# Writing the steps of a pipelined transformer stage out, and forming the product with V over 64 rows from two arrangements of V

## The chip, the core and the metric

The kernel runs on one core of a Trainium2 chip. The metric is the device time of one execution in microseconds (us), of which several runs are taken; 4808 to 4830 us is what the runs of the kernel before show. The program is written by hand for the five engines of the core: TensorE (PE, matmuls, with its weight loads as PEld), VectorE (DVE), ScalarE (ACT), GpSimd (POOL) and SyncE (SP, which issues the DMAs here). Each engine has a queue of its own, and the engines wait for each other through semaphores.

## What is computed

The reference is a chain of small networks over one input of 16 sequences of 256 tokens with 128 channels. The part that the change touches is a transformer of six layers with attention in windows of 32 tokens; a window sees its own tokens and those of the window before:

```python
def local_attention(q, k, v):            # 16 heads of 64 columns, w = 32
    ...
    bq = q.reshape(b, h, nw, w, d)
    ...
    def look(t):                         # the window before, zeros in front of a sequence
        p = jnp.pad(t, ((0, 0), (0, 0), (1, 0), (0, 0), (0, 0)))
        return jnp.concatenate([p[:, :, :nw], p[:, :, 1:]], axis=3)
    bk2, bv2 = (look(bk), look(bv))
    ...
    sim = jnp.einsum('bhwie,bhwje->bhwij', bq, bk2) * QK_SCALE
    sim = jnp.where(mask, -jnp.finfo(sim.dtype).max, sim)
    attn = jax.nn.softmax(sim, -1)
    out = jnp.einsum('bhwij,bhwje->bhwie', attn, bv2)
```

Ahead of the attention, half of the channels are shifted by one token, q and k are normalised and rotated; behind it come the output product, a residual sum, and a gated feed-forward layer. The product `bhwij,bhwje->bhwie` (probabilities by values, 64 keys for each of 32 queries) is called the product with V below. The other networks (one in front, four behind) are not touched.

## The kernel before, in words

The transformer stage works on tiles of 128 tokens: two tiles are one sequence of one layer (a unit), so that 16 sequences and 6 layers make 96 units and 192 tiles. It is a software pipeline of steps. In step k TensorE projects q and k of tile k (`project`, L1071), turns q and k of tile k-1 (`turn_part`, transposes at L1053), makes masks and scores of tile k-2 (`scores`, L1102 and L1112), projects v of tile k-2 (`project_v`, L1087), turns the probabilities of tile k-3 and forms its product with V (`attend`, L1144), and forms the output product of tile k-4 (L1167). The feed-forward layer takes two units at a time, spread over four steps (`widen` and `narrow`, L1189 and L1203). So TensorE's work repeats every four steps. VectorE rotates and makes the softmax's sums, GpSimd sums the rotated parts and scales, ScalarE squares, exponentiates and copies PSUM banks to SBUF: o of tile k-3 (`keep_out`), V of tile k-2 (`keep_v`, L1275, from the bank that the scores also use), q and k of tile k-1.

The order on each engine is written out by hand (`body(step)` of each engine). The first 16 steps and the last 16 are written out; the eleven rounds of 16 steps between run in a hardware loop (`all_steps`, L773), in which each engine's waits are against values computed in its registers from the round. `Event.at` gives such a value; `place` numbers the fills of the turning bank.

The probabilities of a tile lie in `probT` with the keys on the partitions: the 64 keys of a window at rows 0 to 63 for the even heads and 64 to 127 for the odd ones. The keys stand by their row modulo 64, so in every second window the own window is the lower half and the window before the upper half, and in the others the other way round. `V` holds the values likewise, 64 rows of two windows for even and for odd heads, in four slots for four tiles. `attend(step, parity)` works on 32 rows of V at a time: a slice of V of one window serves its own window and the next (64 moving columns), or one of them alone (32 columns) at a tile's edge. Both calls add into the same PSUM bank, which two priming matmuls with zeros (L1131) have opened. The first call (32 matmuls) stands before the transposes of k of the next tile, the second (32 for an even tile, 48 for an odd one, which has the slice of the tile before to add) behind them, with a wait for the first.

SP's queue carries, for each unit: the shifted output (`shift_output`, L897 to L899), the residual (L891), the input with its shift (L886 to L888), and every second unit the saved z (L904). At a layer's end SP loads the next layer's weights in parts and gives each free by an event (`q_ok` for the q columns, `k_ok`, `v_ok`, `out_ok` for Wo, `ff_ok`), in between waiting for their last readers.

Of the kernel before, what the change touches and what calls it, by code (L numbers as in the profile page):

```python
# [16 lines left out]
P = 128  # L17
# [652 lines left out]
LOOP = 16  # L670
# [16 lines left out]
class Step:  # L687
# [12 lines left out]
    def v_slot(self, lag):  # L700

        return (self.k - lag) % 4
# [5 lines left out]
    def has(self, lag):  # L708
        return not isinstance(self.I, int) or 0 <= self.tile(lag) < TILES

    def has_input(self):
        return self.k % 2 == 1 and (not isinstance(self.I, int) or self.tile(0) < TILES)
# [5 lines left out]
    def has_pair(self):  # L718
        return not isinstance(self.I, int) or 0 <= self.pair() < UNITS // 2
# [41 lines left out]
def place(step, name):  # L761

    if isinstance(step.I, int) and step.I == 0:
        return FIRST_FILLS[step.k, name]
    if isinstance(step.I, int) and step.I == ROUNDS:
        return LAST_FILLS[step.k, name]
# [3 lines left out]
def all_steps(engine, body):  # L770
    for k in range(LOOP):
        body(Step(0, k))
    with engine.Fori(1, ROUNDS) as I:  # L773
        for k in range(LOOP):
            body(Step(I, k))
    for k in range(LOOP):
        body(Step(ROUNDS, k))


def transformer_stage(k, z):  # L780

    nc, d = k.nc, k.dram
    with ExitStack() as ctx:
# [14 lines left out]
        zerob = sb("zerob", [P, P], BF16)  # L798
# [12 lines left out]
        V = sb("V", [P, 4, WPT // 2, PAIRS, HD])  # L811
# [38 lines left out]
        v_done, v_kept, pv_done = ev("v_done"), ev("v_kept"), ev("pv_done", 2)  # L850
# [8 lines left out]
        def _(sp):  # L859
            for e in (zu_ready, zr_ready[0], zr_ready[1], zsh_ready, z_saved, q_ok, k_ok, v_ok, out_ok, ff_ok):  # L860
                e.start(sp)
# [30 lines left out]

            def shift_output(U, unit):
# [12 lines left out]
            sp.wait_ge(zeroed, 5)  # L906
# [23 lines left out]
            def unit(U):  # L930
# [23 lines left out]
                if U:  # L954
                    sp.sem_inc(v_ok.sem, 1)
                if U + 2 <= UNITS:
# [34 lines left out]
        def _(pool):  # L991
# [7 lines left out]
            pool.wait_ge(zeroed, 4)  # L999
# [44 lines left out]
            all_steps(pool, body)  # L1044

        @block.tensor
        def _(pe):
# [13 lines left out]
            def project(step, kind):  # L1061
                tau, t = step.tile(0), step.t(0)
                if t == 0:
                    e = k_ok if kind else q_ok
                    pe.wait_ge(e.sem, e.at(step.I * (LOOP // 2) + step.k // 2, 1))
                    if kind == 0 and not (isinstance(step.I, int) and tau == 0):
# [56 lines left out]
            def attend(step, parity):  # L1123
# [1690 lines left out]
```

## Time and profile before

| | |
|---|---|
| median of 3 runs | 4816.22 us (4808.3 to 4830.12) |
| the profiled execution's own time | 4819.65 us |
| its span in the trace | 4817.9 us |
| transformer stage in the trace | about 210 to 3626 us |
| TensorE busy | 4398.4 us, 91% of the span |
| VectorE busy | 3142.6 us, 65% |
| ScalarE busy | 2723.2 us, 57% |
| GpSimd busy | 2626.5 us, 55% |

The times of single instructions come from the profiled execution, whose span begins 1.8 us short of its time. A float32 matmul leaves two records in the trace, so a group "x64" is 32 matmuls. Matmuls overlap, so what one costs is the distance from its start to the next one's start and not its own length. The granted clock of TensorE is given as a share of its full speed: 1.00 is the 2.4 GHz level, 0.50 the 1.2 GHz level. Idle time in brackets is what the engine stood still before the row, with what ended it; "issue" means that the profile shows nothing that it waited for.

### The profile page before, as it was taken

To read this page: it belongs to the slowest core of one execution; us is meant where nothing else is said; L and a number is where in the kernel's file an instruction comes from. 1 tells how busy PE (TensorE), PEld (TensorE's weight loads), DVE (VectorE), ACT (ScalarE), POOL (GpSimd) and SP (SyncE) were. 2 spreads that over 40 slices of the span, in tenths; PEclk is the share of its full clock that TensorE was granted. 3 is DMA by queue.
4 is the path that set the end of the run, shared out by engine and by line. 5 is a ranking of instruction groups with operands and counts; after the bars stand their busy time and mean duration, and the time that the engine had idled before them with its cause. 6 is when DMAs were issued, how large, how long until landed. Compare 5 with 4: busy or idle time off the path is not lost. (4 is left out here: it accounts for less than half of the span.)

```text
span 4817.9 us, 164830 instructions
## 1 busy us (share of the span) xinstructions
PE 4398.4 (91%) x72648; PEld 2863.6 (59%) x72648; DVE 3142.6 (65%) x4111; ACT 2723.2 (57%) x3930; POOL 2626.5 (55%) x1467
## 2 busy tenths in 40 slices
PE   7489999999999999999999999999984999788878
PEld 5256666666666666666666666666652555344435
DVE  3477676767667666667666676766743443599974
ACT  4246665656666565566656665665652444577743
POOL 0266665666666665666666665666632212477752
PEclk8599999999999999999999999999995999799989
DMA  2100001000100001100010001000001000211100
GB/s 55 51 11 16 19 20 37 20 20 18 30 24 25 18 18 33 27 20 15 20 37 23 17 20 29 24 24 18 19 14 33 1 1 1 87 76 71 71 34 16
DMA packets 184442, 134.16 MB, mean 28 GB/s; under 512 B 122296, under 2 KB 170433, under 8 KB 181633
## 3 DMA queue, kind: packets, MB, share of 16 engines
q1 hardware_dynamic: 183681, 122.99, 8.5%
q8 instruction: 602, 9.86, 0.9%
q14 instruction: 159, 1.30, 0.1%
HBM read 68.50 MB, written 4.03 MB: 15 GB/s over the span
## 5 line engine op out<-in xcount | busy, mean ns | idle before, releaser
L1005 POOL TENSOR_TENSOR tf_qk<-tf_qk,tf_rot 128x1024 f32<-128x1024 f32 x384 | 908.9, 2367 | 1221.8 <-DVE tf_rot L1388 1221.8
L1071 PE MATMUL tf_psum<-tf_Wqkv,tf_xsT 128*128 128x512 f32 x1536 | 749.6, 611 | 66.9 <-issue 46.5
L1012 POOL TENSOR_TENSOR tf_qk<-tf_qk,tf_rn 128x1024 f32<-128x1024 f32 x384 | 724.3, 1913 | 53.5 <-ACT tf_rn L1271 53.4
L1264 ACT ACTIVATE tf_sq<-tf_psum 128x1024 f32<-128x1024 f32 x384 | 393.4, 1025 | 533.7 <-DVE tf_rot L1388 533.7
L1384 DVE TENSOR_TENSOR tf_qk<-tf_psum,tf_table 128x1024 f32<-128x1024 f32 x384 | 467.4, 1217 | 265.3 <-PE tf_psum L1071 264.6
L1144 PE MATMUL tf_psum<-tf_probT,tf_V 32*64 32x64 f32 (+1 forms) x27648 | 494.1, 219 | 7.0 <-issue 6.6
L1071 PEld LDWEIGHTS tf_psum<-tf_Wqkv,tf_xsT 128*128 128x128 f32 x1536 | 273.4, 193 | 350.1 <-issue 339.3
L1394 DVE TENSOR_REDUCE tf_ss<-tf_sq 128x16 f32<-128x1024 f32 x384 | 457.6, 1192 | 21.3 <-ACT tf_sq L1264 21.3
L1144 PEld LDWEIGHTS tf_psum<-tf_probT,tf_V 32*64 32x64 f32 x27648 | 443.4, 133 | 45.7 <-issue 40.4
L1388 DVE TENSOR_TENSOR tf_rot<-tf_psum,tf_table 128x1024 f32<-128x1024 f32 x384 | 465.7, 1213 | 0.0
L1053 PE MATMUL tf_psum<-ident,tf_qk 128*128 128x128 f32 x3072 | 408.5, 276 | 3.4 <-ACT tf_qT L1283 2.4
L1053 PEld LDWEIGHTS tf_psum<-ident,tf_qk 128*128 128x128 f32 x3072 | 343.3, 141 | 102.4 <-issue 81.8
L1447 DVE SCALAR_TENSOR_TENSOR tf_hT<-tf_psum,tf_b,tf_gel 128x512 f32<-128x512 f32 x144 | 107.5, 746 | 435.9 <-ACT tf_gel L1316 435.9
L1167 PE MATMUL tf_psum<-tf_Wo,tf_oT 128*128 128x128 f32 x3072 | 376.3, 275 | 7.4 <-issue 4.4
L1167 PEld LDWEIGHTS tf_psum<-tf_Wo,tf_oT 128*128 128x128 f32 x3072 | 362.3, 192 | 31.8 <-issue 21.2
L1020 POOL TENSOR_TENSOR tf_prob<-tf_prob,tf_rden 128x1024 f32<-128x1024 f32 x192 | 367.2, 1913 | 13.2 <-DVE tf_rden L1418 13.2
L1087 PE MATMUL tf_psum<-tf_Wqkv,tf_xsT 128*32 128x512 f32 x3072 | 369.4, 598 | 0.0
L1283 ACT ACTIVATE tf_qT<-tf_psum 128x1024 f32<-128x1024 f32 x192 | 196.7, 1024 | 282.9 <-PE tf_psum L1053 282.9
L2001 POOL TENSOR_TENSOR mb_read<-mb_state,mb_Csb 128x1024 f32<-128x1024 f32 x128 | 300.4, 2357 | 75.5 <-DVE mb_state L2244 55.3
L1112 PEld LDWEIGHTS tf_psum<-tf_kT,tf_qT 64*32 64x32 f32 x24576 | 262.5, 106 | 110.8 <-issue 110.6
L1112 PE MATMUL tf_psum<-tf_kT,tf_qT 64*32 64x64 f32 x24576 | 298.0, 228 | 21.0 <-issue 20.9
L2084 PE MATMUL mb_psum<-mb_read,ident 128*128 128x512 f32 x512 | 253.5, 618 | 56.0 <-POOL mb_read L2001 44.9
(319 smaller groups left out, 7483.8 us busy)
## 6 DMA issues: line engine op xcount, KB each, us to landing
mb_Csb<-mb_kept SPq DMA_DIRECT2D x16, 2048.0 KB, 7.1
tf_zr<-z SPq DMA_DIRECT2D x96, 128.0 KB, 2.7
z<-tf_z SPq DMA_DIRECT2D x48, 256.0 KB, 2.5
tf_Wqkv<-in_Wqkv_split SPq DMA_DIRECT2D x18, 512.0 KB, 3.7
tf_zu<-z SPq DMA_DIRECT2D x97, 64.0 KB
tf_zu<-z SPq DMA_DIRECT2D x97, 63.5 KB
tf_zsh<-tf_z SPq DMA_DIRECT2D x96, 64.0 KB
tf_zsh<-tf_z SPq DMA_DIRECT2D x96, 63.5 KB
```

The lines of the kernel that those rows point to most:

```text
L1005: nc.gpsimd.tensor_tensor(v, v, rot[:, kind, :], ALU.add).then_inc(added.sem, 1)
L1012: nc.gpsimd.tensor_tensor(v, v, rn[:, t, HEADS * kind:HEADS * (kind + 1)].unsqueeze(2) .to_broadcast([P, HEADS, HD]), ALU.mult).then_inc(n ...
L1053: last = nc.tensor.transpose(flat2(trans)[:, j * P:(j + 1) * P], source(j), k.ident[:, :])
L1071: last = nc.tensor.matmul(proj[:, half, :], xsT[:, step.unit(0), WIN + t * P:WIN + (t + 1) * P], Wqkv[:, c:c + 512], start=True, stop=True)
L1087: last = nc.tensor.matmul(score[r:r + 32, m, :], xsT[:, step.unit(2), x:x + WIN], Wqkv[:, c:c + 512], start=True, stop=True)
L1112: last = nc.tensor.matmul(score[w * WIN:(w + 1) * WIN, odd, pair * HD:(pair + 1) * HD], qT[r, t, pair, w * WIN:(w + 1) * WIN], keys, start ...
L1144: last = nc.tensor.matmul(mixed[64 * half:64 * half + 64, odd, j * P + lo:j * P + hi], V[r, step.v_slot(3 + back), v // 2, pair, :], probT ...
L1167: last = nc.tensor.matmul(mixed[:, 0, 0:P], oT[:, t, pair, :], Wo[:, pair, :], start=(pair == 0), stop=(pair == PAIRS - 1))
L1264: nc.scalar.activation(sq[:, kind, :], flat2(proj), ACT.Square).then_inc(squared.sem, 1)
L1384: nc.vector.tensor_tensor(qk[:, t, kind, :].rearrange("p (h e) -> p h e", e=HD), v, cos, ALU.mult)
L1388: nc.vector.tensor_tensor(rot[:, kind, :].rearrange("p (h a e) -> p h a e", a=2, e=HD // 2), swapped, sin, ALU.mult).then_inc(roped.sem, 1)
L1394: nc.vector.tensor_reduce(ss[:, t, HEADS * kind:HEADS * (kind + 1), 0], sq[:, kind, :].rearrange("p (h e) -> p h e", e=HD), AX.X, ALU.add)\
```

## The change

The change has two parts.

First, the loop is gone: all 192 + 16 steps are written out on every engine, and all waits are against constants.

Second, there are two arrangements of V. `V` is as before, with two slots instead of four, and serves the odd windows of a tile; `Vback` holds the values moved by one window, so that the 64 rows of an even window (its own and the one before) stand in it in the order of `probT`'s rows. Every window's product is now one matmul over 64 rows with 32 moving columns, 64 matmuls for each tile, in one call without priming and without a second addition into the bank. `Vback` is laid by SP with copies from SBUF to SBUF, `lay_back`: four of them for an even tile, six for an odd one (two more bring over the last window of the tile before). Window 0 of an even tile is the start of a sequence; its rows of the window before are zeros, set once by GpSimd and never written again. `attend` waits for the copies (`laid`), the copies wait for V (`v_kept`) and for the product of the tile two before (`pv_done`), and `keep_v` waits for the copies of the tile before (`laid`) and for the product of the tile that had its slot. The whole product stands before the transposes of k.

```diff
-def all_steps(engine, body):
-    for k in range(LOOP):
-        body(Step(0, k))
-    with engine.Fori(1, ROUNDS) as I:
-        for k in range(LOOP):
-            body(Step(I, k))
-    for k in range(LOOP):
-        body(Step(ROUNDS, k))
+def all_steps(body):
+    for n in range((ROUNDS + 1) * LOOP):
+        body(Step(n // LOOP, n % LOOP))
...
-        V = sb("V", [P, 4, WPT // 2, PAIRS, HD])
+        V, Vback = (sb(n, [P, TT, WPT // 2, PAIRS, HD]) for n in ("V", "Vback"))
...
-        v_done, v_kept, pv_done = ev("v_done"), ev("v_kept"), ev("pv_done", 2)
+        v_done, v_kept, pv_done, laid = ev("v_done"), ev("v_kept"), ev("pv_done"), [ev("laid0", 64), ev("laid1", 96)]
...
+            def lay_back(tau):
+
+                t = tau % 2
+                sp.wait_ge(v_kept.sem, v_kept.at(tau, 1))
+                sp.wait_ge(pv_done.sem, pv_done.at(tau - 2, 1))
+                for odd in range(2):
+                    even_rows, odd_rows = (slice(64 * odd + i, 64 * odd + i + WIN) for i in (0, WIN))
+                    sp.dma_start(Vback[even_rows, t, :, :, :], V[even_rows, t, :, :, :]).then_inc(laid[t].sem, 16)
+                    sp.dma_start(Vback[odd_rows, t, 1, :, :], V[odd_rows, t, 0, :, :]).then_inc(laid[t].sem, 16)
+                    if t:
+                        sp.dma_start(Vback[odd_rows, 1, 0, :, :], V[odd_rows, 0, 1, :, :]).then_inc(laid[1].sem, 16)
...
                 if U:
                     sp.sem_inc(v_ok.sem, 1)
+                if U:
+                    lay_back(U * 2 - 1)
...
             for U in range(UNITS):
+                if U:
+                    lay_back(U * 2 - 2)
                 if U >= 2:
                     residual(U)
                 unit(U)
+            lay_back(TILES - 2)
+            lay_back(TILES - 1)
...
-            pool.wait_ge(zeroed, 4)
+            nc.gpsimd.memset(Vback[:, 0, 0, :, :], 0.0).then_inc(zeroed, 1)
+            pool.wait_ge(zeroed, 5)
...
+            def attend(step):
 
                 tau, t = step.tile(3), step.t(3)
-                if parity == 0:
-                    pe.wait_ge(copied, place(step, "p") + 2)
-                    pe.wait_ge(v_kept.sem, v_kept.at(tau, 1))
-                    pe.wait_ge(z_added.sem, z_added.at(tau - 1, 1))
-                    for odd in range(2):
-                        nc.tensor.matmul(mixed[:, odd, 0:1], zerob[:, :], identb[:, 0:1],
-                                         start=True, stop=False, skip_group_check=True)
-                    windows = [(0, 0), (2, 0)]
-                else:
-                    pe.wait_ge(pv_done.sem, pv_done.at(tau, 1))
-                    windows = [(1, 0), (3, 0)] + ([(3, 1)] if t else [])
+                pe.wait_ge(copied, place(step, "p") + 2)
+                pe.wait_ge(laid[t].sem, laid[t].at(step.unit_of(3), 96 if t else 64))
+                pe.wait_ge(z_added.sem, z_added.at(tau - 1, 1))
                 for j in range(PAIRS // 2):
-                    for v, back in windows:
-                        lo, hi = (0, WIN) if back else (v * WIN, min(v + 2, WPT) * WIN)
+                    for w in range(WPT):
+                        source = V if w % 2 else Vback
                         for half in range(2):
                             for odd in range(2):
-                                r = slice(64 * odd + 32 * parity, 64 * odd + 32 * parity + 32)
-                                pair = j + 4 * half
-                                last = nc.tensor.matmul(mixed[64 * half:64 * half + 64, odd, j * P + lo:j * P + hi],
-                                                        V[r, step.v_slot(3 + back), v // 2, pair, :],
-                                                        probT[r, t, pair, lo:hi],
-                                                        start=False, stop=True, skip_group_check=True)
+                                r = slice(64 * odd, 64 * odd + 2 * WIN)
+                                pair, at = j + 4 * half, w * WIN
+                                last = nc.tensor.matmul(mixed[64 * half:64 * half + 64, odd, j * P + at:j * P + at + WIN],
+                                                        source[r, t, w // 2, pair, :], probT[r, t, pair, at:at + WIN],
+                                                        start=True, stop=True)
                 last.then_inc(pv_done.sem, 1)
...
                 if step.has(1):
                     turn_part(step, 0)
                 if step.has(3):
-                    attend(step, 0)
+                    attend(step)
                 if step.has(1):
                     turn_part(step, 1)
-                if step.has(3):
-                    attend(step, 1)
...
             def keep_v(step):
+                t = step.t(2)
                 act.wait_ge(v_done.sem, v_done.at(step.tile(2), 1))
-                nc.scalar.activation(V[:, step.v_slot(2), :, :, :].rearrange("p m a e -> p (m a e)"), flat2(score), ACT.Copy)\
+                act.wait_ge(laid[1 - t].sem, laid[1 - t].at(step.unit_of(3), 64 if t else 96))
+                act.wait_ge(pv_done.sem, pv_done.at(step.tile(4), 1))
+                nc.scalar.activation(V[:, t, :, :, :].rearrange("p m a e -> p (m a e)"), flat2(score), ACT.Copy)\
                     .then_inc(v_kept.sem, 1)
...
             def keep_out(step):
-                act.wait_ge(pv_done.sem, pv_done.at(step.tile(3), 2))
+                act.wait_ge(pv_done.sem, pv_done.at(step.tile(3), 1))
...
-            nc.vector.memset(zerob[:, :], 0.0).then_inc(masks_ready, 1)
```

Three places of the order show what moves. The first is TensorE's order in the loop before, around the product of an odd tile; `tf_qk` is q or k, whose transposes are L1053, L1131 is the priming, L1144 the product, "x32" the number of matmuls in a row, REGISTER_ALU rows compute values to wait for, and the shapes are rows of the result by moving columns:

```order
L1053 MATMUL tf_psum<-ident,tf_qk 128x128 [waits tf_copied]
L1053 MATMUL tf_psum<-ident,tf_qk 128x128 x7
L1131 MATMUL tf_psum<-tf_identb,tf_zerob 128x1 [waits tf_z_added,tf_v_kept,tf_copied]
L1131 MATMUL tf_psum<-tf_identb,tf_zerob 128x1
L1144 MATMUL tf_psum<-tf_probT,tf_V 64x64 x32
L1093 REGISTER_ALU
L1094 REGISTER_ALU [waits tf_normed]
L1053 MATMUL tf_psum<-ident,tf_qk 128x128 [waits tf_copied]
L1053 MATMUL tf_psum<-ident,tf_qk 128x128 x7
L1144 MATMUL tf_psum<-tf_probT,tf_V 64x64 [waits tf_pv_done]
L1144 MATMUL tf_psum<-tf_probT,tf_V 64x64 x3
L1144 MATMUL tf_psum<-tf_probT,tf_V 64x32 x8
```

The same place in the order of the changed kernel; L1066 are the transposes and L1149 the product, whose groups of four go on alternating until 64 matmuls are made, and then the transposes of k follow:

```order
L1066 MATMUL tf_psum<-ident,tf_qk 128x128 [waits tf_copied,tf_normed]
L1066 MATMUL tf_psum<-ident,tf_qk 128x128 x7
L1149 MATMUL tf_psum<-tf_probT,tf_Vback 64x32 [waits tf_z_added,tf_laid1,tf_copied]
L1149 MATMUL tf_psum<-tf_probT,tf_Vback 64x32 x3
L1149 MATMUL tf_psum<-tf_probT,tf_V 64x32 x4
L1149 MATMUL tf_psum<-tf_probT,tf_Vback 64x32 x4
L1149 MATMUL tf_psum<-tf_probT,tf_V 64x32 x4
L1149 MATMUL tf_psum<-tf_probT,tf_Vback 64x32 x4
L1149 MATMUL tf_psum<-tf_probT,tf_V 64x32 x4
```

The priming and the wait for `pv_done` in the middle are gone, the waits for `z_added` and `copied` stay at the front with `laid` in place of `v_kept`, and the second half of the product has moved ahead of the transposes of k. The last place is SP's queue for one unit, before:

```order
L897 DMA tf_zsh<-tf_z 128x2x64 [waits tf_z_added]
L898 DMA tf_zsh<-tf_z 127x2x64
L899 DMA tf_zsh<-tf_z 1x16x4
L891 DMA tf_zr<-z 128x256
L886 DMA tf_zu<-z 128x2x64 [waits tf_filled]
L887 DMA tf_zu<-z 127x2x64
L888 DMA tf_zu<-z 1x16x4
```

And the same in the changed kernel (L903 to L905 are the shifted output, L885 the residual; the input's three, L880 to L882, follow):

```order
L894 DMA tf_Vback<-tf_V 32x1024 [waits tf_pv_done,tf_v_kept]
L895 DMA tf_Vback<-tf_V 32x512
L894 DMA tf_Vback<-tf_V 32x1024
L895 DMA tf_Vback<-tf_V 32x512
L903 DMA tf_zsh<-tf_z 128x2x64 [waits tf_z_added]
L904 DMA tf_zsh<-tf_z 127x2x64
L905 DMA tf_zsh<-tf_z 1x16x4
L885 DMA tf_zr<-z 128x256
L894 DMA tf_Vback<-tf_V 32x1024 [waits tf_pv_done,tf_v_kept]
L895 DMA tf_Vback<-tf_V 32x512
L897 DMA tf_Vback<-tf_V 32x512
```

Ten copies have come in for each unit: four ahead of the shifted output and six ahead of the next input, each group behind a wait for V's copy and an earlier product.

## Rows read from the trace of the kernel before

**Rows 1.** The page: busy time of each engine, and the scores' group

```profile
PE 4398.4 (91%) x72648; PEld 2863.6 (59%) x72648; DVE 3142.6 (65%) x4111; ACT 2723.2 (57%) x3930; POOL 2626.5 (55%) x1467
...
L1112 PE MATMUL tf_psum<-tf_kT,tf_qT 64*32 64x64 f32 x24576 | 298.0, 228 | 21.0 <-issue 20.9
```

**Rows 2.** Windows of four steps: us, each engine's busy time, PEclk, DMA share, GB/s

```profile
417.84:485.28 67.44, 66.80 (x1406) 46.29 (x1405) 48.18 (x61) 42.35 (x52) 43.41 (x23) 1.00 0.07 18
620.29:688.77 68.48, 67.45 (x1406) 46.57 (x1405) 48.25 (x61) 42.45 (x52) 43.36 (x23) 1.00 0.07 18
688.77:760.82 72.05, 67.61 (x1406) 46.55 (x1404) 49.14 (x63) 42.45 (x52) 43.90 (x23) 1.00 0.11 29
760.82:832.00 71.18, 69.09 (x1404) 47.07 (x1404) 48.54 (x63) 42.34 (x52) 43.34 (x22) 0.98 0.14 38
```

**Rows 3.** Ten windows, one for each loop round from tile 16 to 176: their sum

```profile
sum 2792.31, PE 2714.16 PEld 1866.07 DVE 1934.18 ACT 1697.56 POOL 1734.12; mean PE 271.42 PEld 186.61 DVE 193.42 ACT 169.76 POOL 173.41
```

**Rows 4.** Timeline of TensorE, 1676 to 1711 us: start, length, operation, records

```profile
1677.86 0.19 PE L1131 MATMUL tf_psum<-tf_identb,tf_zerob 128*128 128x1 bf16 x2
1677.98 1.16 PE L1144 MATMUL tf_psum<-tf_probT,tf_V 32*64 32x64 f32 x64
...
1680.16 1.60 PE L1144 MATMUL tf_psum<-tf_probT,tf_V 32*64 32x64 f32 x96
1681.69 1.92 PE L1087 MATMUL tf_psum<-tf_Wqkv,tf_xsT 128*32 128x512 f32 x16
...
1685.80 0.59 PE L1102 MATMUL tf_psum<-tf_mask,tf_identb 128*128 128x512 bf16 x2
1686.33 1.48 PE L1112 MATMUL tf_psum<-tf_kT,tf_qT 64*32 64x64 f32 x128
...
1693.39 0.19 PE L1131 MATMUL tf_psum<-tf_identb,tf_zerob 128*128 128x1 bf16 x2
...
1695.69 1.13 PE L1144 MATMUL tf_psum<-tf_probT,tf_V 32*64 32x64 f32 x64
1696.76 1.92 PE L1087 MATMUL tf_psum<-tf_Wqkv,tf_xsT 128*32 128x512 f32 x16
...
1709.65 0.19 PE L1131 MATMUL tf_psum<-tf_identb,tf_zerob 128*128 128x1 bf16 x2
```

**Rows 5.** The branch (min/median/max ns), TensorE's timeline behind it, and a window

```profile
L773 PEldq COMPARE_BRANCH  x11: 83/4022/5318, 755.4 to 3549.8; - x11
...
1599.00 2.43 PE L1071 MATMUL tf_psum<-tf_Wqkv,tf_xsT 128*128 128x512 f32 x4 [2.05 <-issue]
...
1606.33 1.60 PE L1167 MATMUL tf_psum<-tf_Wo,tf_oT 128*128 128x128 f32 x12 [0.64 <-issue]
...
1600.40:1603.80 3.40, 3.40 (x116) 1.82 (x115) 3.26 (x11) 0.50 (x2) 0.00 (x0) 0.50 0.09 25
```

**Rows 6.** Timeline of SP and TensorE at two layers' ends

```profile
1871.78 0.52 SPq L868 DMA_DIRECT2D tf_Wqkv<-in_Wqkv_split  x1
1871.98 2.84 PE L1203 MATMUL tf_psum<-tf_W,tf_hT 128*128 128x128 f32 x24
...
1876.45 0.33 SPq L868 DMA_DIRECT2D tf_Wqkv<-in_Wqkv_split  x1
...
1389.49 3.77 PE L1071 MATMUL tf_psum<-tf_Wqkv,tf_xsT 128*128 128x512 f32 x4 [2.58 <-SPq L941]
```

**Rows 7.** Timeline of TensorE, 334 to 339 us, in the first written-out part

```profile
337.85 0.33 PE L1112 MATMUL tf_psum<-tf_kT,tf_qT 64*32 64x64 f32 x12 [1.52 <-issue]
```

**Rows 8.** Timeline of SP's issues, 2011 to 2017 us

```profile
2011.74 0.65 SPq L897 DMA_DIRECT2D tf_zsh<-tf_z  x1
2012.43 0.70 SPq L898 DMA_DIRECT2D tf_zsh<-tf_z  x1
2013.17 2.92 SPq L899 DMA_DIRECT2D tf_zsh<-tf_z  x1
```

**Rows 9.** The page's DMA issues: KB each, us to landing

```profile
tf_zr<-z SPq DMA_DIRECT2D x96, 128.0 KB, 2.7
```

**Rows 10.** Timeline of ScalarE, 1676 to 1702 us: the copies to V

```profile
1683.68 1.02 ACT L1275 ACTIVATE tf_V<-tf_psum 128x1024 f32<-128x1024 f32 x1 [0.45 <-PE tf_psum L1087]
...
1698.75 1.02 ACT L1275 ACTIVATE tf_V<-tf_psum 128x1024 f32<-128x1024 f32 x1 [0.31 <-PE tf_psum L1087]
```

More of the change, by code:

```diff
@@ L698, in t, with unit_of @@
         return (self.k - lag) % TT
-    def v_slot(self, lag):
-        return (self.k - lag) % 4
+    def unit_of(self, lag):
+        return self.I * (LOOP // 2) + (self.k - lag) // 2
     def unit(self, lag):
@@ L708, in has @@
     def has(self, lag):
-        return not isinstance(self.I, int) or 0 <= self.tile(lag) < TILES
+        return 0 <= self.tile(lag) < TILES
     def has_input(self):
-        return self.k % 2 == 1 and (not isinstance(self.I, int) or self.tile(0) < TILES)
+        return self.k % 2 == 1 and (self.tile(0) < TILES)
     def pair(self):
@@ L718, in has_pair @@
     def has_pair(self):
-        return not isinstance(self.I, int) or 0 <= self.pair() < UNITS // 2
+        return 0 <= self.pair() < UNITS // 2
     def before(self):
@@ L761, in place @@
 def place(step, name):
-    if isinstance(step.I, int) and step.I == 0:
+    if step.I == 0:
         return FIRST_FILLS[step.k, name]
-    if isinstance(step.I, int) and step.I == ROUNDS:
+    if step.I == ROUNDS:
         return LAST_FILLS[step.k, name]
     return (step.I - 1) * ROUND_FILLS + (LOOP_START + LOOP_FILLS[step.k, name])
-def all_steps(engine, body):
-    for k in range(LOOP):
-        body(Step(0, k))
-    with engine.Fori(1, ROUNDS) as I:
-        for k in range(LOOP):
-            body(Step(I, k))
-    for k in range(LOOP):
-        body(Step(ROUNDS, k))
+def all_steps(body):
+    for n in range((ROUNDS + 1) * LOOP):
+        body(Step(n // LOOP, n % LOOP))
 def transformer_stage(k, z):
@@ L859, in _ @@
         def _(sp):
-            for e in (zu_ready, zr_ready[0], zr_ready[1], zsh_ready, z_saved, q_ok, k_ok, v_ok, out_ok, ff_ok):
+            for e in (zu_ready, zr_ready[0], zr_ready[1], laid[0], laid[1], zsh_ready, z_saved, q_ok, k_ok, v_ok, out_ok, ff_ok):
                 e.start(sp)
@@ L1042, in body @@
                     weigh(step)
-            all_steps(pool, body)
+            all_steps(body)
         @block.tensor
@@ L1065, in project @@
                     pe.wait_ge(e.sem, e.at(step.I * (LOOP // 2) + step.k // 2, 1))
-                    if kind == 0 and not (isinstance(step.I, int) and tau == 0):
+                    if kind == 0 and tau:
                         pe.wait_ge(copied, place(step.before(), "input") + 2)
@@ L1242, in body @@
                     narrow(step)
-            pe.wait_ge(zeroed, 5)
-            pe.wait_ge(masks_ready, 5)
+            pe.wait_ge(zeroed, 6)
+            pe.wait_ge(masks_ready, 4)
             turn_input(0, 0)
             pe.wait_ge(copied, 2)
-            all_steps(pe, body)
+            all_steps(body)
         @block.scalar
@@ L1356, in _ @@
             copy_input(0, 0)
-            all_steps(act, body)
+            all_steps(body)
         @block.vector
```

8 lines of the change are left out of this document (3 added, 5 removed).

## Prediction

> **What bounds the kernel now.** The page comes first: TensorE is busy for 91% of the span, no other engine for more than 65% [rows 1]. That is an average over five stages and a busy TensorE may still be waiting inside a matmul, so the transformer stage is read next in stretches of four steps, one full pattern (TensorE's work repeats every four tiles). A stretch in the written-out part takes 67.44 us, of which TensorE is busy 66.80 and VectorE, the next, 48.18 [rows 2]. There are 48 such stretches. TensorE's own order therefore sets the pace, and a microsecond taken from its stream is a microsecond of the end, as long as nobody becomes late in its place. Two stretches of [rows 2] are much longer, 72.05 and 71.18 us: the last of a loop round and the first of the next. The ten rounds between the starts of tiles 16 and 176 take 2792.31 us [rows 3], 279.2 each, against 4 x 67.44 = 269.8: 9.5 us a round is lost, some 8 of it next to the branch. Both parts of the change aim at TensorE: one shortens its stream, the other removes the branch.
>
> **The product with V.** The rows of [rows 4] give distances from start to start, which is what pipelined matmuls cost. For an odd tile: 1677.86 to 1681.69, 3.83 us for priming, first half, second transpose and second half; for an even tile 1693.39 to 1696.76, 3.37 us. The first half ends at 1677.98 + 1.16 = 1679.14 and the second begins at 1680.16: the transposes of k between them are 1.02. What does one product cost? 64 records (32 matmuls; a float32 matmul leaves two records) go in 1.16 us when all have 64 columns, and 64 of which half have 32 columns go in 1.13; 96, two thirds of them with 32 columns, take 1.53 to the next start (1680.16 to 1681.69). In a block of 64 the first record and the hand-over to the next group cost some 0.2, the rest is 14.5 to 15 ns a record whether 32 or 64 columns pass. So the number of records counts, not the columns: four tiles of the array are in flight at a time, before as after, and each turns around in some 4 x 14.5 = 58 ns. The change makes 64 matmuls, 128 records, for every tile, in place of 128 and 160. 128 x 14.5 = 1.86, plus 0.17 of hand-over, makes 2.03; the transpose adds 1.00. 3.03 against 3.37 and 3.83 saves 0.34 and 0.80, 0.57 on average, and over 192 tiles **109 us**.
>
> No row has a 64 x 64 tile in float32. The bounds are from the nearest rows: the scores (64 rows, 32 stationary columns, eight tiles) need 1.48 us for 128 records, about 10 ns [rows 4], which would make 1.28 + 0.17 and save another 0.58 x 192 = 111 us; and twice the present turnaround, 29 ns, would cost 1.86 x 192 = 357 us more. I take 14.5, because the stationary width is that of today's product and the tiles in flight are four in both.
>
> A rule speaks against this. First the row: 32-row tiles at 14.5 to 15 ns a record [rows 4]. TensorEngine Tiling, section Performance Considerations, in the Trainium skill, says that a contraction of 32 gets four-fold row tiling and one of 64 only two-fold; by it the new product loses half of the array's tiles. But the code's 32-row slices of one call lie at rows 0 and 64, or 32 and 96: half of the row groups rest, and the trace agrees, since eight tiles in flight would show twice the pace. The other way that rule gives is rival C.
>
> **The branch.** At the end of a round TensorE's branch takes 4022 ns in the median [rows 5]. It is issued ahead of the queued matmuls, so 2.05 us of idle time are seen; then the granted clock is 0.50, the 1.2 GHz level, for 3.40 us, which costs 1.7 of the 2.4 GHz work, and a further stall of 0.64 falls in the output product [rows 5]. Together 4.4 us at each of the five branches inside a layer: 22 us, all given back. (Runtime: NRT & Kernel Launch, section Instruction fetch mechanics, in the Trainium skill, says that a taken branch out of the fetched window waits for a DMA fetch and that full unrolling avoids it; by that rule all 4.4 would return, as in my sum.) The other five fall on a layer's end, and there another wait stands behind: SP issues the q columns at 1871.78 and gives q_ok only just before its next issue at 1876.45, while TensorE's narrow product ended at 1871.98 + 2.84 = 1874.8 [rows 6]. Without a branch TensorE still waits 1.6, and about 2.0 since it comes sooner; after the 2.58 us wait for SP at 1389.49 the four records of a projection took 3.77 us, twice what 512 columns need elsewhere, so the slow clock probably comes too, 1.7. The two stretches of [rows 2] lose 72.05 + 71.18 - 134.9 = 8.3 us, 2 of them ordinary stalls of the size of the 68.48 one; of the other 6.3 some 3.7 stay, 2.6 x 5 = 13 are gained. Branches: **35 us**. Register instructions go too; TensorE shows no wait for them, so I cost them at nothing.
>
> **The instruction stream.** Straight code is still read from memory. In it the scores, the densest instructions, can stall: 1.52 us once in the written-out part [rows 7]; all stalls inside the scores (L1112) sum to 21.0 us [rows 1]. A clean stretch has none, another 1.04 more (68.48 against 67.44, [rows 2]). The new product is a second dense run, 256 instructions in 2.0 us, split today by a transpose. I take the present loss, since positions no longer repeat, with 20 us to either side.
>
> **The copies.** Every tile adds 4 (even) or 6 (odd) copies on SP's queue, between v's copy to V and the product. Short issues on SP take 0.33 to 0.70 us [rows 6, 8], and a copy of 128 KB, as large as the largest of the new ones, lands after 2.7 [rows 9]. Six take 2.0 to 4.2 plus the landing, at most 6.9; four at most 5.5. The time they have: V is copied by 1684.70 and the even tile's product begins 1693.39, 8.7 us later; 1699.77 to 1709.65, 9.9, for an odd one [rows 4, 10]. They are hidden under projection, scores and output product, with 3 us to spare. Queued behind them on SP are the next input (needed two steps later), the save of z and q_ok; per pair of tiles they add up to 7 us of issues to a queue that has 33.7 (half of 67.44) for two triples and two or three more, some 9 us by [rows 8]. If that cover is gone, each microsecond is one per tile, 192 in all. Only after a layer's end, where SP sits in weight waits, may a product wait: 5 x 1 us, and the Wo wait (2.58) grows by 0.4: together **5 us** lost. V has two slots now, so ScalarE's copy waits for copies issued one step earlier, long landed; behind it stand the input copy and gelu.
>
> ScalarE is next in line if anything is: k's copy now starts after the whole product, so o's copy and V's follow up to 0.8 us later, while TensorE's next scores want V's copy out of the bank. V's copy ended at 1684.70 [rows 10], 1.1 us before the masks that open the scores (1685.80, [rows 4]); 0.8 later leaves 0.3. Cost nothing, little margin.
>
> **Sum.** 109 + 35 - 5 = 139. Against the profiled run's own 4819.65 us that is 4681; its time is 3.4 over the median of 4816.22, so 4677, said as **4680 us**.
>
> **Rivals.**
> A. Another chain takes part of the gain: V's copy ends late, and the scores wait 0.4 us a step, 77 us; 4757. For: the margin of 0.3. Against: 48 of 67 us of VectorE, 42 of ScalarE [rows 2]. With it counts any partial gain, 4725 to 4792: 0.17.
> B. The copies issue slowly, slower than before. The third copy of a triple takes 2.92 us [rows 8]. At 2.9 each, six need 17.4 + 2.7 = 20.1 us where 9.9 are there, and SP's ten per pair make 29 + 9 = 38 us a pair against 33.7 now: 96 x 4.3 = 413 us over today's 4816, 5229. It decides from (9.9 - 2.7)/6 = 1.2 us an issue. Against: the slow one always follows a copy of 127 partitions; the new ones are even, 32 rows each, like the short ones. 0.05.
> C. The 64-row tiles are slower, 29 ns a record: 4680 + 357 = 5037; at 20 ns, +135, 4815, no change. Slower from there. It counts also for an instruction stream that starves at every scores and product (1.52 x 192 = 292: 4972). Together 0.08.
> D. The product goes at the scores' 10 ns: 4680 - 111 = 4569. For: its rows may have been bound by half-used row groups. 0.06.
> No change to tell: 0.04.
>
> **Numbers.** A measurement of this kernel tells from about 0.5%, 24 us. My forecast, 4640 to 4725, has 0.60; A 0.17, B 0.05, C 0.08, D 0.06, no change 0.04. The range 4630 to 4770 holds the forecast and most of A, leaving out B, C, no change, D. Faster 0.84, same 0.04, slower 0.12.
>
> **What would show it.** Right: 128 records with 32 columns in about 2.0 us for every tile; a stretch of four steps at about 65.2 us; no 4 us branch and no slow clock inside a layer; waits for laid absent or at layer ends. Wrong: a record pitch of 20 ns or more, idle time of the product that a DMA of Vback ends, more stalls at the scores, or SP still issuing Vback copies when the next z_added has come.

## The result and the profile after

The changed kernel takes 4771.7 us (4770.2 to 4776.0, four runs) against 4813.5 of the kernel before in the same comparison: 0.991 of it, 95% interval 0.989 to 0.993. That is 42 us less, where 139 were forecast; the range ended at 4770. All runs below were timed beside the kernel before, which had medians of 4809 to 4812 us.

First the page of the changed kernel, then the same four stretches of four steps as in [rows 2], and then its ten times sixteen steps from tile 16 to tile 176 in one window, which answer to [rows 3]:

```profile
PE 4331.5 (91%) x69192; PEld 2789.7 (58%) x69192; DVE 3143.9 (66%) x4110; ACT 2702.9 (57%) x3930; POOL 2624.7 (55%) x1468
```

```profile
421.25:487.32 66.07, 65.42 (x1334) 44.66 (x1333) 48.21 (x61) 41.94 (x52) 43.27 (x23) 1.00 0.20 46
623.82:690.27 66.45, 65.98 (x1335) 45.06 (x1333) 48.27 (x61) 41.95 (x52) 43.32 (x23) 1.00 0.20 46
690.27:760.12 69.85, 67.01 (x1334) 45.01 (x1333) 49.64 (x66) 42.08 (x52) 44.77 (x23) 1.00 0.21 52
760.12:829.00 68.88, 66.27 (x1333) 45.08 (x1333) 48.05 (x61) 41.97 (x52) 43.41 (x22) 1.00 0.28 69
...
487.32:3230.32 2743.00, 2659.91 (x53282) 1805.34 (x53281) 1932.15 (x2440) 1680.10 (x2080) 1732.23 (x881) 0.99 0.21 50
```

The 160 tiles take 2743.0 us in place of 2792.3, so 49 us came in there by these two profiles. A single profile carries some chance: behind the transformer stage, where neither kernel was changed, the profiled executions took 1141.4 us before and 1131.6 after, and 1132 to 1141 in the runs below. The best stretch has gone from 67.44 to 66.07, not to 65.2. The DMA engines are busy 20 to 28% of the time in these stretches, where [rows 2] had 7 to 14%.

TensorE's timeline for one even tile has the new product just as forecast:

```profile
2091.24 1.04 PE L1066 MATMUL tf_psum<-ident,tf_qk 128*128 128x128 f32 x8
2092.20 0.32 PE L1149 MATMUL tf_psum<-tf_probT,tf_Vback 64*64 64x32 f32 x8
...
2093.97 0.30 PE L1149 MATMUL tf_psum<-tf_probT,tf_V 64*64 64x32 f32 x8
2094.20 1.09 PE L1066 MATMUL tf_psum<-ident,tf_qk 128*128 128x128 f32 x8
2095.22 1.92 PE L1100 MATMUL tf_psum<-tf_Wqkv,tf_xsT 128*32 128x512 f32 x16
```

From 2092.20 to 2095.22 product and second transpose take 3.02 us (3.03 forecast), and records go at (2093.97 - 2092.20) / 120 = 14.7 ns. But the transposes of q ahead of it now take 0.97 from start to start (median of 160), where those ahead of the priming took 0.87: a hand-over that I had not counted.

The waits of TensorE from 480 to 3450 us (engine, line, releaser: us in all, times, longest) show what is new:

```profile
PE tf_psum L1149 <- issue: 30.0, 25, 2.3
PE tf_psum L1125 <- issue: 13.8, 12, 1.9
PE tf_psum L1149 <- DVE tf_z L1433: 13.6, 39, 0.4
PE tf_psum L1193 <- ACT tf_oT L1303: 11.4, 43, 0.3
PE tf_psum L1084 <- SPq L947: 9.0, 7, 1.6
```

In the kernel before, the product had 5.3 us of idle time without a releaser, the feed-forward's first product (L1193 here) never waited for o's copy, and the branch had 26.5. The timeline of the worst kind of stall:

```profile
1025.52 0.33 PE L1149 MATMUL tf_psum<-tf_probT,tf_Vback 64*64 64x32 f32 x8
1028.16 0.44 PE L1149 MATMUL tf_psum<-tf_probT,tf_V 64*64 64x32 f32 x8 [2.32 <-issue]
1028.53 1.97 PE L1066 MATMUL tf_psum<-ident,tf_qk 128*128 128x128 f32 x8
```

and the window right behind it, with the granted clock third from the end:

```profile
1027.80:1031.20 3.40, 3.04 (x20) 2.07 (x23) 0.00 (x0) 0.66 (x1) 0.05 (x1) 0.50 0.19 53
```

The last eight records of a product come 2.3 us late, and about the end of that stall the granted clock falls to 0.50, the 1.2 GHz level, for 3.4 us: the transposes take 1.97 instead of 1.09. Stretches at the half clock make up 47.8 us between tiles 16 and 176, in twelve places, 44.4 in ten before. For the most part they have only changed their place: eight of the ten stood at a branch, and all twelve now stand at a stall of the product, eleven inside it and one in front.

### The profile page after: what moved, and what is told of

Same layout as the page of the kernel before. It is cut to its first block and busy times, and to the rows that moved or that the text cites. A ratio compares the mean times of both kernels' runs of the same rounds, so it can differ in the third digit from the quotient of the medians.

```text
span 4771.0 us, 155839 instructions
## 1 busy us (share of the span) xinstructions
PE 4331.5 (91%) x69192; PEld 2789.7 (58%) x69192; DVE 3143.9 (66%) x4110; ACT 2702.9 (57%) x3930; POOL 2624.7 (55%) x1468
## 5 line engine op out<-in xcount | busy, mean ns | idle before, releaser
L1084 PE MATMUL tf_psum<-tf_Wqkv,tf_xsT 128*128 128x512 f32 x1536 | 737.6, 603 | 41.5 <-issue 20.6
L1066 PE MATMUL tf_psum<-ident,tf_qk 128*128 128x128 f32 x3072 | 416.4, 279 | 7.3 <-issue 4.9
L1149 PE MATMUL tf_psum<-tf_probT,tf_Vback 64*64 64x32 f32 x12288 | 383.3, 221 | 29.8 <-DVE tf_z L1433 15.6
L1066 PEld LDWEIGHTS tf_psum<-ident,tf_qk 128*128 128x128 f32 x3072 | 349.1, 143 | 95.4 <-issue 87.5
L1149 PE MATMUL tf_psum<-tf_probT,tf_V 64*64 64x32 f32 x12288 | 382.8, 220 | 23.8 <-issue 23.7
L1100 PE MATMUL tf_psum<-tf_Wqkv,tf_xsT 128*32 128x512 f32 x3072 | 387.1, 620 | 0.0
L1149 PEld LDWEIGHTS tf_psum<-tf_probT,tf_Vback 64*64 64x64 f32 x12288 | 340.8, 135 | 65.4 <-issue 62.7
L1149 PEld LDWEIGHTS tf_psum<-tf_probT,tf_V 64*64 64x64 f32 x12288 | 343.5, 136 | 24.0 <-issue 23.9
```

What stands on the lines that cost most here:

```text
L1066: last = nc.tensor.transpose(flat2(trans)[:, j * P:(j + 1) * P], source(j), k.ident[:, :])
L1084: last = nc.tensor.matmul(proj[:, half, :], xsT[:, step.unit(0), WIN + t * P:WIN + (t + 1) * P], Wqkv[:, c:c + 512], start=True, stop=True)
L1100: last = nc.tensor.matmul(score[r:r + 32, m, :], xsT[:, step.unit(2), x:x + WIN], Wqkv[:, c:c + 512], start=True, stop=True)
L1149: last = nc.tensor.matmul(mixed[64 * half:64 * half + 64, odd, j * P + at:j * P + at + WIN], source[r, t, w // 2, pair, :], probT[r, t, pa ...
```

## The experiments

**One part alone.** `e1_unrolled` is the kernel before with nothing but

```diff
...
-    with engine.Fori(1, ROUNDS) as I:
-        for k in range(LOOP):
-            body(Step(I, k))
...
+    for n in range((ROUNDS + 1) * LOOP):
+        body(Step(n // LOOP, n % LOOP))
```

> The kernel before with all steps written out and nothing else changed. Theory: writing out gives back what stood at the ten branches of the loop between tiles 16 and 176, 26.8 us of idle time and ten stretches of 3.4 us at the half clock (17 us), some 44 us, and the stalls without a releaser in the changed kernel's product with V belong to the new product: 4770 us, the product with V keeps its few stalls (7 us in all). Rival: straight code stalls as such, and the 35 us of stalls in the product come from writing out: 4795 to 4810 us, with more than 20 us of stalls at the product or the scores.

Measured: 4774.1 us, ratio 0.994 (0.992 to 0.996), 36 us less. Its ten times sixteen steps:

```profile
486.30:3230.20 2743.90, 2687.71 (x56162) 1857.82 (x56161) 1930.29 (x2440) 1694.96 (x2080) 1732.96 (x881) 1.00 0.09 23
```

One stretch at the half clock is left, at 1928.2, behind a wait for SP at a layer's end. Writing out alone gives what the whole change gave, within the noise.

`e2_loop_kept` is the other part alone, the new product in the old loop, with the two priming matmuls put back ahead of it to carry the wait:

```diff
...
+                for odd in range(2):
+                    nc.tensor.matmul(mixed[:, odd, 0:1], zerob[:, :], identb[:, 0:1],
+                                     start=True, stop=False, skip_group_check=True)
                 for j in range(PAIRS // 2):
```

> The changed kernel with the loop of 16 steps put back; ahead of each product stand the two priming matmuls of the kernel before, which only carry the wait. The product is 0.47 us a tile shorter than before by the changed kernel's rows, 0.12 of which the priming takes back: 192 x 0.35 = 67 us. Theory: the dense product stalls here too wherever its code lies badly, 20 us or more, and widen waits 13 us for o's copy, so only 20 to 35 us remain: 4780 to 4795 us. Rival: the stalls come only with written-out code: 4813 - 67 + 13 + 10 = 4770 us or less, no stalls over 1 us in the product.

Measured: 4808.6 us, ratio 0.9998 (0.9986 to 1.0011): no gain at all. In its waits the scores (L1131 there) stand first, and the branch (L1090) is as before:

```profile
PE tf_psum L1131 <- issue: 31.5, 33, 1.7
PE tf_psum L1090 <- issue: 27.6, 10, 3.6
...
PE tf_psum L1158 <- issue: 14.4, 14, 1.5
```

The product's block is shorter as computed (422 us with priming for 160 tiles before, 361 here), the scores and v's projection take 43 us of it back, 13 of them in front of the widening, which here too waits for o's copy. The ten rounds are 18 us shorter in this profile, which the medians don't show; both theories missed, and neither named the scores.

**Where the stalls come from.** `e3_split` puts the transposes of k between two halves of the product:

```diff
-                    attend(step)
+                    attend(step, 0)
                 if step.has(1):
                     turn_part(step, 1)
+                if step.has(3):
+                    attend(step, 1)
```

> The changed kernel with the transposes of k between the two halves of the product, 32 matmuls each. Theory: the stalls come where a long run of short matmuls uses its instructions up faster than they are fetched; halves with the slow transposes between them stall seldom. Gone: 28 of the 35 us of stalls, the slow clock behind them (12 stretches of 3.4 us, 20 us), the wait of widen for o's copy (13 us). Added: two hand-overs, 0.13 us a tile, 26 us. 4772 - 61 + 26 = 4737 us. Rival: the stalls depend on the copies or on the code's place alone, and stay: 4772 - 13 + 26 = 4785 us.

Measured: 4745.8 us, ratio 0.987 (0.985 to 0.989). Call a stall of the product a distance of over 0.5 us between the starts of two neighbouring records inside it. The changed kernel has 15 of them, 29.3 us in all and up to 2.5 each; here there are 16, but of 1.2 us at most and 14.9 in all, and the half-clock stretches fall from twelve to one. So the split makes the stalls shorter, not fewer. The rival, 4785, is out. The 26 us are not the price of the stalls alone: k's transposes stand between the halves again, and with them the wait for o's copy in front of the widening is gone too (13.4 us over 160 tiles, see `e5_o_first`), while the added hand-overs cost something.

The trace of the changed kernel shows that the place in the code matters. The long stalls at every eighth tile, with the record in the product at which each stands:

```text
tile    44   52   60 |  88   96  104  112 | 132  140  148  156
record 120  109   98 | 124  113  102   91 | 127  116  105   94
```

Within each of the three groups the place lies 11 records earlier every eight tiles, and no stall of the product lies before record 90. In the loop kernels it is the same record in each round (116 and 125 in `e2_loop_kept`'s scores, 89 and 112 before).

**What the copies cost.** `e4_no_copies` leaves the copies out, Vback is zero:

```diff
             def lay_back(tau):
+                return
...
-                pe.wait_ge(laid[t].sem, laid[t].at(step.unit_of(3), 96 if t else 64))
+                pe.wait_ge(v_kept.sem, v_kept.at(tau, 1))
```

> The changed kernel without the copies to Vback, which is set to zero once, so that the even windows are multiplied by zeros; the product waits for V's copy instead. Theory: the copies cost nothing but the wait at the end of the stage (6.7 us, and 1.5 to 3 of slow clock behind it): 4762 us, the same 35 us of stalls in the product. Rival: the copies' traffic holds up the fetches of instructions, and the stalls and the slow clock behind them go with it: 4772 - 10 - 28 - 20 = 4714 us.

Measured: 4725.9 us, ratio 0.9835 (0.982 to 0.985). 46 us less: my theory (4762) fell, and the rival (4714) is nearly right.

```profile
481.02:3177.67 2696.65, 2631.02 (x53283) 1788.85 (x53281) 1927.11 (x2440) 1678.36 (x2080) 1733.15 (x881) 1.00 0.09 24
```

Of the table above the stalls at records 98, 102, 91 and 94 are gone, those at 105 and later stay; in all 15 stalls of the product have become 8, and the half-clock stretches 5 in place of 12. At tile 60 the instruction fetches (16 KB each, on their own queue) begin, in us from the product's start:

```text
with copies      -16.8   -9.9           +1.0   +5.4    stall of 2.1 at record 98
without copies   -16.7  -10.5   -2.6    +2.5           none
```

With copies the fetch that otherwise begins ahead of the product begins inside it, and the stall ends 2.6 us after that. The copies are not the whole reason, though. At the places from record 109 on, a fetch begins 1.0 to 1.8 us into the product with copies and without, and the stall is there in both. And in `e13_no_copies_o_first` below, which has no copies either, the stalls of tiles 60 and 112 (records 98 and 91) are back at 2.1 and 1.9 us, with the fetch at +0.9. So between records 91 and 105 it can go either way: of six such places (tiles 16, 60, 104, 112, 148, 156) the changed kernel stalls at all six, this run at one and `e13_no_copies_o_first` at two. The other part is fine-grained: the scores lose 13 us over 160 tiles, 11 of them in distances of 0.02 to 0.12 us.

Four runs ask how. `e7_copies_twice` makes each copy again into a spare buffer; `e8_dram_copies` makes the same copies from DRAM to DRAM; `e9_copies_unwaited` copies V into a buffer that no engine waits for; `e14_small_copies` does the same with 64 columns of each row (the labels at the ends of the lines are not in the code):

```diff
-                for odd in range(2):                                   # e7
+                for to, odd in ((Vback, 0), (Vback, 1), (Vtwo, 0), (Vtwo, 1)):
...
-                    sp.dma_start(Vback[even_rows, t, :, :, :], V[even_rows, t, :, :, :])
+                    sp.dma_start(sink[t, odd, 0, :, :], from_)         # e8
+                    sp.dma_start(Vtwo[even_rows, t, :, :, :], V[even_rows, t, :, :, :])   # e9
+                    sp.dma_start(Vtwo[even_rows, t, 0, 0:1, 0:64], V[even_rows, t, 0, 0:1, 0:64])   # e14
```

In the last three Vback is zero, as without copies; the product still waits for the copies' landing in `e8_dram_copies`, and not in the other two.

> The changed kernel with every copy to Vback made a second time into a buffer that nobody reads; the product waits for all of them. The copies were found to cost 46 us although nothing on TensorE waits for them. Theory: it is their traffic that costs, so twice the traffic costs about twice: 4772 + 46 = 4818 us, with more stalls without a releaser on TensorE, and SP's queue still in time. Rival: the cost comes from the waits for laid or from something that happens once a tile, so more copies are free until the product waits for them: 4772 to 4780 us.

Measured: 4932.7 us, ratio 1.0245 (1.022 to 1.027), 161 more than with single copies. The product now also waits for the landing, so this is no price of traffic alone:

```profile
PE tf_psum L1150 <- issue: 103.0, 79, 5.5
```

> The changed kernel with as many copies of the same sizes at the same places, but from DRAM to DRAM, so that SBUF is not touched; Vback is zero and the even windows are multiplied by zeros. Theory A: the copies hold up the fetches of instructions, which go over the same DMA engines: as slow as the changed kernel, 4772 us, with its 50 us of stalls at product and scores. Theory B: they disturb TensorE's reads and the engines' writes of SBUF: 4726 us as without copies, plus 9 us for the wait at the stage's end, 4735 us.

Measured: 4766.6 us, ratio 0.990 (0.987 to 0.992), near theory A and 41 above the run without copies, so most of the cost comes without SBUF being touched.

> The changed kernel with the same copies out of V, but into a buffer that the product doesn't read; Vback is zero, the even windows are multiplied by zeros, and the product waits for V's copy alone. Without copies it was 4726 us, with them 4772. Theory: the copies' traffic costs, not a wait for them: 4766 to 4772 us. Rival: the product's wait for the copies' landing is what costs, shown without a releaser at the product: 4726 to 4735 us.

Measured: 4755.8 us, ratio 0.988 (0.9865 to 0.9895). 30 of the 46 us come with copies that no product waits for; it falls 10 below the theory's figure. The 30 hold the stage's end (below), where SP's order is that of the changed kernel: from tile 191's start to the next stage 153.7 us, where `e4_no_copies` has 144.2. Some 20 are left for the traffic.

The other 16 come with the wait for the landing. In the changed kernel products behind a layer's end show it, here in the timelines of SP and TensorE:

```profile
1865.41 0.59 SPq L897 DMA_DIRECT2D tf_Vback<-tf_V  x1
...
1867.48 0.44 PE L1149 MATMUL tf_psum<-tf_probT,tf_Vback 64*64 64x32 f32 x8 [1.99 <-ACT tf_qT L1288]
```

The last copy's issue ends at 1866.00 and the product starts 1.48 later. The q copy that the row names is not what it waits for, since other products start 0.2 us behind q's transposes. The products of tiles 29, 93, 125 and 157 start 3.2 us late in all, and none of them in `e4_no_copies` or `e9_copies_unwaited`. The half-clock stretches, 47.8 us against 30.7 of `e9_copies_unwaited`, cost 8.5 more, one of them behind this very wait.

> As the run whose copies nobody waits for (4756 us, against 4726 without copies), but each copy moves 64 columns of its 32 rows, 8 KB in place of 128 or 64 KB. Theory: the bytes on the DMA engines hold up the instruction fetches: 4726 to 4736 us, the latter with the wait at the stage's end. Rival: the number of copies, or what SP issues, is what disturbs: 4750 to 4756 us as before.

Measured: 4743.0 us, ratio 0.986 (0.983 to 0.988), between the two. From tile 16 to 176:

```profile
483.90:3212.70 2728.80, 2652.50 (x53282) 1801.03 (x53281) 1932.85 (x2440) 1679.83 (x2080) 1731.97 (x881) 0.99 0.21 50
```

```profile
488.49:3201.28 2712.79, 2648.45 (x53283) 1800.49 (x53281) 1931.73 (x2440) 1680.39 (x2080) 1732.40 (x881) 0.99 0.10 26
```

2728.8 with full copies that nothing waits for, 2712.8 with small ones, 2696.7 with none: half goes with the number of copies and half with their bytes (both sides of each step by one profile, so several us may be chance).

**ScalarE's order.** The timeline of ScalarE and TensorE behind a product that ended near 1973.4, in the changed kernel:

```profile
1974.52 1.02 ACT L1288 ACTIVATE tf_kT<-tf_psum 128x1024 f32<-128x1024 f32 x1 [0.67 <-PE tf_psum L1066]
1975.44 1.02 ACT L1303 ACTIVATE tf_oT<-tf_psum 128x1024 f32<-128x1024 f32 x1
...
1976.60 1.95 PE L1193 MATMUL tf_psum<-tf_xnT,tf_W 128*128 128x512 f32 x4 [0.27 <-ACT tf_oT L1303]
```

o's bank is done before the transposes of k start, but its copy stands behind k's, which now comes 1 us later; widen needs the bank. `e5_o_first`:

```diff
+                if step.has(3):
+                    keep_out(step)
                 if step.has(1):
                     copy_part(step, 1)
-                if step.has(3):
-                    keep_out(step)
```

> The changed kernel with ScalarE's copy of o ahead of its copy of k. Theory: the product now ends before the transposes of k, so o's copy only stands behind k's by the order of the queue, and widen waits for it; the 13.5 us of that wait go, and nothing takes their place, since k's copy is needed only by the next step's scores: 4772 - 13 = 4759 us. Rival: k's copy comes 1 us later and V's copy behind both as before, but the transposing bank is free later, so TensorE waits there instead: 4772 us.

Measured: 4728.0 us, ratio 0.982 (0.9795 to 0.984), 44 less and not 13. By the distances from start to start over 160 tiles, 13.4 us are the wait in front of the first widening and 6 the hand-overs and starts near it; the other 17 of the 36 gained there lie in stalls and half-clock stretches (nine instead of twelve), which came at other moments.

**The end of the stage.** SP's and TensorE's timelines of the changed kernel:

```profile
3528.69 0.51 SPq L894 DMA_DIRECT2D tf_Vback<-tf_V  x1
...
3533.93 2.96 SPq L905 DMA_DIRECT2D tf_zsh<-tf_z  x1
...
3537.05 3.44 PE L1171 MATMUL tf_psum<-tf_Wo,tf_oT 128*128 128x128 f32 x16 [6.68 <-SPq L996]
```

The copies of the last tile stand ahead of the shifted output whose `out_ok` the last output products want. `e6_tail` puts them in the order of all other units:

```diff
-            lay_back(TILES - 2)
-            lay_back(TILES - 1)
             for i in range(2):
+                lay_back(TILES + i - 2)
                 shift_output(UNITS + i - 2, i + 2)
```

> The changed kernel with the last two units of SP's queue in the order of all the others: the copies of the last tile stand behind the shifted output that frees the last output product. Theory: the wait of 6.7 us for SP at the stage's end goes, with some of the slow clock behind it (the output product took 3.44 us instead of 1.95): 4764 us. Rival: the product with V of the last tile is late in its place, since its copies now stand behind the three of the shifted output (4.4 us): 4772 us.

Measured: 4763.8 us, ratio 0.990 (0.988 to 0.992); from tile 191's start to the next stage 145.8 us instead of 156.3 (144.1 before). The medians differ by 8 us, with intervals of the two ratios that overlap; that the wait is gone is shown by the trace.

**Together.** `e10_o_first_tail` and `e11_split_tail` combine these edits. `e12_copies_after_scores` adds to the first of them

```diff
+                if t == 0:
+                    sp.wait_ge(scored.sem, scored.at(tau + 1, 1))
```

> The changed kernel with o's copy ahead of k's and the stage's end in order. The two cures touch different waits (44 us and 8 us measured one by one), so they add: 4728 - 8 = 4720 us. Rival: part of the 44 us was the luck of the slow stretches, as only 13 us of them were a wait: 4740 us.

Measured: 4724.6 us, ratio 0.983 (0.981 to 0.985), nearer to the theory, though only 3 below `e5_o_first`, which is within the noise.

> The changed kernel with the product in two halves around the transposes of k, and the stage's end in order: 4746 - 8 = 4738 us, by the theory that the halves trade long stalls for hand-overs. Rival: the last tiles' stalls move and nothing is won: 4746 us.

Measured: 4739.6 us, ratio 0.985 (0.984 to 0.987), 2 from the theory.

> The kernel with o's copy first and the end in order, and in addition the four copies of every even tile wait for the scores of the next tile, so that they don't run beside these short matmuls. Theory: what the copies cost lies partly in the scores (13 us more in 160 tiles than without copies), and half of it goes: 6 to 8 us less than with the copies at once, 4712 us. Rival: the copies disturb whatever runs beside them, or come late for the product: 4720 to 4730 us.

Measured: 4723.1 us, ratio 0.983 (0.981 to 0.985): no difference to `e10_o_first_tail`. The scores did become 10 us shorter over 160 tiles, but the product has 25 gaps of over 0.15 us inside in place of 15, and 4 us more. The copies seem to disturb whatever runs beside and behind them.

`e13_no_copies_o_first` has the edits of `e4_no_copies` and `e5_o_first`, the even windows multiplied by zeros.

> No copies (Vback is zero, the even windows are multiplied by zeros) and o's copy ahead of k's: the two cures that gave 46 and 44 us one by one. Theory: 19 us of the 44 are the wait for o's copy and what stands behind it, and the rest is stalls and slow clock that the missing copies already removed in part: 4726 - 19 to 4726 - 36, so 4690 to 4707 us. Rival: they hit the same stalls, and only the 13 us of the wait are left: 4713 us.

Measured: 4689.6 us, ratio 0.975 (0.972 to 0.978), at the low end of the theory's figures, with 8 stalls of the product (15.8 us) and seven half-clock stretches. A stretch of four steps is then 65.45:

```profile
419.74:485.19 65.45, 65.07 (x1335) 44.56 (x1333) 48.19 (x61) 42.10 (x52) 42.71 (x22) 1.00 0.07 19
```

## Why the prediction was wrong

- **The product with V, 109 us.** Mechanism and pace were right: 14.7 ns a record as in 32-row tiles, 3.02 us a block. Mis-sized by the hand-over ahead of it, 0.09 us a tile, 18 us: 91 remain. Rivals C (by pace) and D are out.
- **The branch, 35 us.** `e1_unrolled` gave 36, which fits better than its parts: I had kept the slow clock at all five layer ends, and one was left, and the profiles before and after that edit differ by 48 us in the ten rounds.
- **"I take the present loss" for the instruction stream** failed. The new product is a run of 128 records without a pause, and a late fetch now hits it for 2 us with 3.4 us of slow clock behind. The halves of the old product, with transposes between them, had kept such stalls short; `e3_split` shows it, with none above 1.2 us.
- **"They are hidden under projection, scores and output product"** failed. I priced the copies by the time until the product needs them, with 5 us for the products behind a layer's end, and that part was right: their waits are 3.2 us. The copies cost 46 us all the same: some 10 at the stage's end, which I had not looked at, some 20 by their traffic, with which instruction fetches come late more often, and 16 that come only when the product waits for them, most of which the 3.2 us and the slow clock account for. It is what rival C had as its second half, an instruction stream that starves, but in one tile of a dozen and not in all.
- **"Cost nothing, little margin" for ScalarE** failed in its place: I watched V's copy and the scores, and the one that came late was o's copy for the feed-forward. Rival A's kind, with another buffer; worth 44 us, of which 19 are the wait itself and the hand-overs near it.
- The sum nearly closes. The copies and ScalarE's order cost 82 us together (46 and 44 one by one; I take it that they share stalls), and 91 + 36 - 82 = 45, where 42 were measured. `e13_no_copies_o_first`, which has neither, gained 122 us on the kernel before, and 91 + 36 = 127. That it lies so near is in part chance, since it has stalls of its own that the sum does not hold.
- A slip in the chances: faster adds up to 0.83 and slower to 0.13, not 0.84 and 0.12.

**Open** is how a copy makes a fetch late (DRAM copies do it too, number and bytes both count), why a stall comes back at the same record without copies, and some 4 of the 16 us between copies that are waited for and copies that are not. That the late fetches are TensorE's is inferred: the rows do not say whose instructions a fetch carries, but each of the 15 stalls ends 2.2 to 3.0 us after one began. Which of the shares of `e5_o_first` beyond the wait is due to its order, and which to the chance of stalls, was not told apart.

## What to carry to other kernels

A transfer that is early enough for its reader may still cost: where an engine works through long runs of short instructions, count the DMAs added per run as a load that may disturb the instruction stream, and try the kernel without them first. Slower work between two halves of such a run halved the stalls here, and left one half-clock stretch of twelve. When one instruction block is moved ahead of another, look at every consumer queue whose order was made for the old sequence. A written-out prologue or end needs the same order as the steady state; check its last unit.

## What the runs showed of the hardware

- Float32 matmuls of 32 moving columns over 64 rows leave records at 14.7 ns, as those over 32 rows did; the number of rows made no difference.
- In the changed kernel TensorE stands still inside a product for up to 2.3 us, seen as "issue", and each of these stalls ends 2.2 to 3.0 us after an instruction fetch begins. Of thirteen waits of 1.5 us or more in or in front of the product between tiles 16 and 176, twelve were followed by 3.4 us or more at a granted clock of 0.50. Stalls in the scores left the clock at 1.00: `e1_unrolled` had nine of 1.0 to 1.5 us, the changed kernel seven of 1.4 to 1.9, from start to start, and no half-clock stretch behind any.
- SBUF copies that nothing waited for cost 30 us in 4756, of which some 10 are SP's order at the stage's end. Copies between DRAM buffers of the same sizes, waited for, cost 41, and SBUF copies that are waited for 46.
